# Four chained graph networks on one core: the written order of steps, one merge for the first five passes, one for the middle, one for the last six

## What is computed

```python
x = _layernorm(x + _L0_gnn_ref(x, adj, ...))
x = _layernorm(x + _L1_gnn_ref(x, adj, ...))
x = _layernorm(x + _L2_gnn_ref(x, adj, ...))
x = _layernorm(x + _L3_gnn_ref(x, adj, nodemask, ...))
```

## Time and profile before

| | |
|---|---|
| median of 3 runs | 1689.47 us (1687.17 to 1689.93) |
| span of the profiled execution, first to last instruction | 1687.2 us |
| TensorE, share of busy time | 96% |
| VectorE | 83% |
| ScalarE | 78% |
| GpSimd | 47% |
| mean granted TensorE clock | 0.995 of full speed |

### The profile page before, as it was taken

The page is one execution under the profiler, slowest core; times in us unless marked ns, Lnnn a source line. Parts: engine busy times, 40 slices in busy tenths (PEclk is TensorE's granted clock), DMA queues, the critical chain, the costliest instruction groups (busy, mean ns, idle before and its releaser), DMA issues.

```text
span 1687.2 us, 34433 instructions
## 1 busy us (share of the span) xinstructions
PE 1619.3 (96%) x12294; PEld 1343.7 (80%) x12294; DVE 1400.9 (83%) x3563; ACT 1314.6 (78%) x3147; POOL 790.3 (47%) x842
## 2 busy tenths in 40 slices
PE   8789999999999999999999999999999999999997
PEld 7568787887878788787887878888787888877776
DVE  5687888979789897989879798897978889797766
ACT  2568878887878888878887887878787888878766
POOL 3143544536454463544546354453645445354442
PEclk9899999999999999999999999999999999999999
DMA  3010100001010100101001010000101001000000
GB/s 95 20 42 1 30 26 17 27 14 42 14 30 14 28 28 14 30 26 30 14 20 36 14 31 26 18 26 14 43 13 30 25 17 27 14 26 14 13 1 20
DMA packets 84803, 40.97 MB, mean 24 GB/s; under 512 B 10629, under 2 KB 84634, under 8 KB 84634
## 3 DMA queue, kind: packets, MB, share of 16 engines
q1 hardware_dynamic: 84058, 38.62, 8.4%
q10 hardware_dynamic: 576, 0.15, 0.0%
HBM read 30.36 MB, written 8.39 MB: 23 GB/s over the span
## 4 chain that ended last, share of the span: by engine, by line
PE 82%; DVE 8%; ACT 7%; issue 1%; POOL 1%; SPq 0%; DMA 0%; POOLq 0%; DVEq 0%; ACTq 0%
PE RA L996 18%; PE RB L996 17%; PE Q L958 8%; PE RT L1193 8%; PE RT L958 4%; PE Q L1107 4%; PE Q L1124 3%; PE M L958 3%; PE Q L1140 2%; ACT x L553 2%; PE Q L1094 2%; PE Q L1090 2%; PE M L1157 2%; PE M L1152 2%; PE Q L1091 2%; PE M L1035 1%
## 5 line engine op out<-in xcount | busy, mean ns | idle before, releaser
L535 POOL TENSOR_TENSOR h_lo<-hT,h_hi 128x512 fp32r<-128x512 f32 (+1 forms) x163 | 205.9, 1264 | 561.0 <-ACT h_hi L636 488.3
L610 ACT ACTIVATE e_s<-Q,s_ng 128x128 f32<-128x128 f32 x1024 | 292.2, 398 | 42.2 <-DVE s_ng L803 42.1
L539 POOL TENSOR_TENSOR hd<-hT,nn 128x512 f32<-128x512 f32 x156 | 201.0, 1288 | 38.7 <-ACT nn L654 38.7
L811 DVE TENSOR_TENSOR p_s<-Q,adjTe 128x512 f32<-128x512 f32 x256 | 171.2, 684 | 15.5 <-PE Q L958 14.3
L803 DVE TENSOR_REDUCE s_ng<-Q 128x4 f32<-128x512 f32 x256 | 169.1, 682 | 14.0 <-PE Q L1107 12.3
L646 ACT ACTIVATE tr<-RA,b_rz 128x512 f32<-128x512 f32 (+1 forms) x160 | 113.7, 710 | 83.6 <-PE RA L996 83.6
L861 DVE SCALAR_TENSOR_TENSOR un<-tr,un 128x512 f32<-128x512 f32 (+1 forms) x164 | 115.1, 704 | 72.2 <-ACT un L650 71.7
L958 PE MATMUL Q<-ident,e_s 128*128 128x128 f32 x1024 | 154.0, 275 | 10.9 <-ACT e_s L610 10.8
L654 ACT ACTIVATE nn<-tr,wT 128x512 f32<-128x512 f32 (+1 forms) x164 | 118.0, 722 | 57.6 <-DVE tr L866 57.5
L958 PEld LDWEIGHTS Q<-ident,e_s 128*128 128x128 f32 x1024 | 122.3, 141 | 33.1 <-ACT e_s L610 16.6
L488 POOL TENSOR_TENSOR rs<-ve,half_neg 128x4 f32<-128x4 f32 x128 | 140.3, 1096 | 10.7
(11 more groups left out here) (237 smaller groups left out, 4429.2 us busy)
## 6 DMA issues: line engine op xcount, KB each, us to landing
...
adjc<-in_adj_dram SPq DMA_DIRECT2D x124, 4.0 KB, 2.1
xs<-in_x_dram SPq DMA_DIRECT2D x120, 16.0 KB, 1.8
...
```

Source lines behind the costliest of these rows:

```text
L535: pool.tensor_tensor(h_lo[g][:, c], hT[g][:, c], h_hi[g][:, c], ALU.subtract).then_inc(SG["h_lo"][g], 1)
L539: pool.tensor_tensor(hd[g][:, c], hT[g][:, c], nn[g][:, c], ALU.subtract).then_inc(SG["hd"][g], 1)
L610: ins = act.activation(e_s[:, j, c, :], Q[j][:, c * P:(c + 1) * P], ACT.Exp, bias=s_ng[:, j, c:c + 1])
L811: dve.tensor_tensor(p_s[:, j, :, :].rearrange("p (b h) q -> p b h q", b=2), Q[j][:, :].rearrange("p (b h q) -> p b h q", b=2, h=2), adjTe[ ...
```

## The change

No step, instruction, wait or transfer is added or removed. What changes is the written order of steps on TensorE, VectorE, ScalarE and GpSimd; SyncE's queue stays as it is. The old table had two strings for each engine, used in all 19 passes. The new one has three for each engine: one merges the steps of passes 0 to 4 together, so that a step of one pass may stand ahead of a step of the pass before; one is used for each of the passes 5 to 12; one merges passes 13 to 18. The three threads are divided into finer lanes, differently on each engine (`lane`): on TensorE the gated thread becomes R, I, Z and T; on the others the two sets of the gated thread become R and S, and maxima, products and parts of thread B get lanes of their own. Only steps that do something on an engine are in its lanes (`KINDS`). The steps that were put off near the end stay put off (`held_back`).

```diff
--- before.py
+++ after.py
@@ -48,15 +48,49 @@
 )
 LAG = 3
 
+HEAD, TAIL = 5, 13
+
 MERGE = dict(
-    tensor=("RRABBARARRBRARABRRRRAABAAARRARRRRAABRARARRRBRBBRBABBRARRRRARARRBBRRRRRRAAAARARABAARRRRBRRRRAAARRRRABBARAAARBBARRARRR",
...
+    tensor=(("BBBBBBBBABABAABBBABAAAAAABAAABAABABAABABABBAABAABABABAABABABAAAATAATARRRBABIZZAABABTABTARRRIAZZABATBTAARBRATRA"
...
 )
 
 
@@ -109,21 +143,84 @@
     return out
 
 
-def body_steps(merge):
-
-    out = []
-    for half in range(NG):
-        threads = dict(A=iter(attention_steps(half)), B=iter(first_third_steps(half)), R=iter(gated_steps(half)))
-        out += [(thread, *next(threads[thread])) for thread in merge[half]]
+THREADS = dict(A=[step for half in range(NG) for step in attention_steps(half)],
+               B=[step for half in range(NG) for step in first_third_steps(half)],
+               R=[step for half in range(NG) for step in gated_steps(half)])
+
+
+KINDS = dict(
...
+)
+
+
+def lane(engine, thread, g, kind):
+
+    if thread == "R" and engine == "tensor":
+        return {"r": "R", "r2": "R", "hn": "R", "in": "I", "z": "Z", "z2": "Z"}.get(kind, "T")
+    if thread == "R":
+        return "RS"[g]
+    if engine == "tensor":
+        return thread
+    if thread == "B":
+        if kind in ("x2", "x2_t", "l2_t", "l2_agg"):
+            return "C"
+        return "B" if kind not in ("adj_t", "l0_add", "x1") else "C" if engine == "vector" else "D"
+    return {"max": "M", "p": "P"}.get(kind, "A")
...
+def near_last(iters):
+    return [(iters - 2, NG - 1), (iters - 1, NG - 2)]
+
+
+def held_back(iters):
+
+    last, (third, second) = (iters - 1, NG - 1), near_last(iters)
...
+def sequence(engine, iters):
+
+    held = held_back(iters).get(engine, {})
+
+    head, body, tail = MERGE[engine]
+    blocks = [(range(HEAD), head)] + [(range(n, n + 1), body) for n in range(HEAD, TAIL)] + [(range(TAIL, iters + LAG), tail)]
+    for passes, merge in blocks:
+        threads = {name: iter([(n, (n - lag, g, kind, k)) for n in passes for lag, g, kind, k in steps if 0 <= n - lag < iters and (n - lag, g, kind, k) not in held])
+                   for name, steps in LANES[engine].items()}
+        for name in merge:
+            yield next(threads[name])
         assert all(next(left, None) is None for left in threads.values())
-    return out
...
@@ -165,20 +262,15 @@
 
         def program(eng, engine, steps, begun=(), first=None):
 
-            for kind in begun:
-                assert (0, kind) in [(lag, kind) for _, lag, g, kind, k in BODY[engine]]
-            held = {}
-            for it in range(ITERS + LAG):
-                for thread, lag, g, kind, k in BODY[engine]:
...
+            after = {}
+            for late, step in held_back(ITERS).get(engine, {}).items():
+                after.setdefault(step, []).append(late)
+            for n, step in sequence(engine, ITERS):
+                if (n == 0 and step[2] in begun) or step == first:
+                    continue
+                steps(*step)
+                for late in after.get(step, ()):
+                    steps(*late)
```

More of the change, by code:

```diff
@@ L118, in body_steps @@
         assert all(next(left, None) is None for left in threads.values())
[L119 to L124 removed]
+SLOTS = [(g, k) for lag, g, kind, k in THREADS["R"] if kind == "agg"]
 BEFORE = {slot: SLOTS[n - 1] for n, slot in enumerate(SLOTS)}
[L126 removed]
+LAG_OF = {(g, k): lag for lag, g, kind, k in THREADS["R"] if kind == "agg"}
@@ L307, in gnn_stack_kernel @@
         LAST = (ITERS - 1, NG - 1)
[L309 to L318 removed]
+        NEAR_LAST = near_last(ITERS)
         def parts(it, g, k):
```

92 lines of the change are left out of this document (63 added, 29 removed).

## The result

| | before | after |
|---|---|---|
| median of 4 runs, us | 1688.32 (1686.72 to 1689.93) | 1705.16 (1702.89 to 1706.32) |
| span of the profiled execution, us | 1687.2 | 1701.0 |
| TensorE busy, us | 1619.3 | 1622.7 |

The change makes the kernel slower: the ratio is 1.0099, 95% interval 1.0085 to 1.0114, that is 16.8 us. The forecast was 8 us shorter. The profiled execution of after is the shortest of its four, so its span shows 13.8 of the 16.8 us.

What follows compares the result with a forecast made beforehand. TensorE was taken as nearly full in the steady part, waiting on chains at both ends. Terms -5.6 + 2.4 + 1.4 - 5.0 - 1.4 = -8.2 us gave a span of 1679.0, with 2.3 added 1681.3, said as 1681; range 1671 to 1692.

Steps and rivals of the forecast that it cites:

- The sum is therefore over places where a wait goes or comes: Whole kernel: all steps, DMAs and waits stay, so only waits that go or come were summed.
- pass 0: Head: three moves shorten the chain of the first attention, -5.6 us; bounds -4 and -8.6.
- pass 2: Head: a_bin of the second four graphs, moved earlier, waits for its adjr load; +2.4 us, range 1.9 to 2.7.
- junctions 12 and 13: Two of ten body-like junctions: projections ahead of the first gated product hide the wait for h_lo, -0.1 us each.
- the 3 us: Slow-clock stretch from 78 to 85 us: up to 3 us more could go; left out of the sum.
- Body-like junctions: Ten junctions, x3 of graphs 4 to 13: o_ts wait replaced by hidden-state wait; +0.2 us in eight, +1.4 in all.
- Junctions of head and tail: Junctions 1, 2, 3, 14, 15: x3 starts at least 0.7 us sooner; -1.0 us each, -5.0 in all.
- Tail: Last x3: y4 goes ahead of un and tr, so it begins sooner; -1.4 us, bounds 0 and -1.4.
- R3: Mid pass: ScalarE's L0 block and normalisation ahead of agg_hi delay a product 1.5 us in ten passes; 1696 us, chance 0.12.

Runs made afterwards that it cites:

- head_first2: The kernel before with the new order in passes 0 and 1 alone; ratio 0.9973 to before, 4.6 us shorter.
- tail_only: The kernel before with the new order in passes 13 to 18 alone; ratio 1.0057 to before, 9.6 us longer.
- tail_pow: tail_only with GpSimd's adjTe, x1b and t_d replaced by powers of few columns lasting about as long; 1695.61 us, ratio 1.0035 to before.
- ends16: head_first2 with the new order also in passes 16 to 18; 1679.20 us, ratio 0.9945 to before.

## Why the prediction was wrong

The step that failed is the one that stands ahead of all terms: "The sum is therefore over places where a wait goes or comes". Terms were booked for pass 0, for pass 2 and for the junctions alone. What lies between the junctions was put at nothing, as if every step lasted as long in its new place as in its old one and TensorE came to every other product as before. Term by term (junction k, the x3 of pass k of the data, lies at the end of pass k+1 of the program):

| part | forecast, us | measured, us |
|---|---|---|
| pass 0 | -5.6 | -3.7 to -4.6 |
| pass 2 | +2.4 | +2.2 |
| from the first hT to that at 427, junctions 1 to 3 | -3.0 | +4.0 |
| passes 5 to 12, eight junctions | +1.6 | +5.2 |
| passes 13 to 15 to hT at 1486, junctions 12 and 13 | -0.2 | +14.1 |
| from there to the end, junctions 14 and 15, last x3 | -3.4 | -5.8 |

**Pass 0, -5.6.** Right in the mechanism and at the low end of its bounds. The product of the values moved from 94.78 to 88.94, but some 1.4 us of that are the clock's; at like clock the order wins 3.7 to 4.4, and head_first2 kept 4.6 by its ratio. The granted clock from 50 to 100 us is 0.93 instead of 0.88, with a new slow stretch (0.63 from 92 to 96). Since kernels of one order differ as much (0.94 and 0.97 up to 115 us in before and tail_only), leaving the 3 us out of the sum was right; here the trace agrees with what the prediction cites.

**Pass 2, +2.4.** Right. a_bin waited 2.77 us for adjr, whose issue moved from 104.59 only to 99.13 while agg_lo moved from 104.84 to 98.52. The load was there 2.86 us after its issue: between the prediction's estimate of 2.6 us, whose section in the Trainium skill is on transfers that GpSimd issues, while SyncE issues this one, and the 3.0 to 3.8 of the earlier trace rows. At either clock the kernels with the new pass 2 stand 2.2 us behind those without it at the first hT (-3.6 against -5.8, -1.5 against -3.7).

**Body-like junctions, +0.14 each.** The junction itself was read rightly: o_ts 1.05 out, hT 0.71 in, and 0.43 of small ones, +0.1 in all. VectorE's sum from hT to nm is the same (4.69 us, before 4.72), and from hT to x3 it takes 5.1 us instead of 4.9, the 0.2 of the forecast. What failed is that nothing was booked for the rest of the pass. There dinv0m, held by t_d, makes the wait of 0.49 for hT; the pass costs 0.6, the body 5.2. With the three GpSimd steps replaced the loss is gone.

**Junctions of head and tail, -1.0 each.** Here too x3 comes sooner behind hT, by 0.3, 0.4 and 0.4 us at junctions 1 to 3 and by 0.7 and 0.4 at 14 and 15 (4.58, 4.53, 4.24, 4.23 and 4.24 us, before 4.91, 4.92, 4.65, 4.92 and 4.65); at four of the five less than the 0.7 forecast. The loss lies between the junctions, where nothing was booked. From the first hT to 427 the head lost 4 us instead of winning 3. With the three steps cut the loss between the same marks is 1.6, so a good half of it is holds. The rest is not settled. Passes 13 to 15 lose 14.1 us. The prediction did not look at them apart from the junctions at all; their merge was new too, and I took them for copies of the steady pass. TensorE's waits there are, besides the 2.42 at 1304.45:

```profile
1435.60 0.70 PE L1097 MATMUL M<-nat,sel 128*128 128x112 f32 x4 [1.11 <-DVE nat L838]
...
1444.51 0.47 PE L1079 MATMUL RA<-agg_hi,comp_hi 128*128 128x512 f32 x1 [1.70 <-DVE agg_lo L939]
...
1480.37 0.47 PE L1079 MATMUL RA<-agg_hi,comp_hi 128*128 128x512 f32 x1 [1.75 <-DVE agg_lo L939]
```

(tail_only.) Each stands behind a VectorE step that is drawn out while GpSimd steps run: a_c 2.43 us instead of 0.60 (beside hd and x1b), x from xin 3.08 instead of 1.11 (beside h_lo and hd), x from y 2.91 instead of 1.11 (beside x1b and hd). The four waits are 7 of the 14.1 us. In tail_pow they are 1.03, gone, 1.67 and 0.91, in the same order. The one that stays whole stands behind the x beside h_lo and hd, the two steps that no kernel here replaced (tail_only, then tail_pow: VectorE, GpSimd, and TensorE's wait in tail_pow):

```profile
1439.49 3.08 DVE L797 TENSOR_SCALAR x<-xin,mv,rs 128x128 f32<-128x128 f32 x4
...
1439.47 1.27 POOL L618 TENSOR_TENSOR h_lo<-hT,h_hi 128x512 fp32r<-128x512 f32 x1 [5.39 <-ACT h_hi L719]
1440.70 1.27 POOL L622 TENSOR_TENSOR hd<-hT,nn 128x512 f32<-128x512 f32 x1
...
1438.67 3.08 DVE L799 TENSOR_SCALAR x<-xin,mv,rs 128x128 f32<-128x128 f32 x4
...
1443.70 0.47 PE L1081 MATMUL RA<-agg_hi,comp_hi 128*128 128x512 f32 x1 [1.67 <-DVE agg_lo L941]
```

So holds by h_lo and hd can make part of the 7.4 us that stay in passes 13 to 15, but this is read from rows and not shown by a run; how much is the order itself stays open.

**Tail, -1.4.** Right in mechanism and size. From the hT ahead of it to the last x3 before needs 4.31 us, after 2.85:

```profile
1621.97 0.69 DVE L879 SCALAR_TENSOR_TENSOR hT<-hd,nn 128x512 f32<-128x512 f32 x1
...
1637.27 0.69 DVE L962 SCALAR_TENSOR_TENSOR hT<-hd,nn 128x512 f32<-128x512 f32 x1
...
1640.12 1.65 ACT L636 ACTIVATE x<-y,nm,rs 128x128 f32<-128x128 f32 x4 [0.97 <-DVE y L969]
```

(The first row is of before, to be read with the earlier trace rows.) Passes 16 to 18 win more than the 2.4 booked for junction 15 and this x3: 4.7 us by the ratios (ends16 against head_first2, 0.9945 and 0.9973), 4.6 in the trace of ends16. Where the rest comes from was not looked into. The last x3 of after is at 1640.12, 13.8 us later than in the earlier trace rows, and from there to the end both kernels need 60.9 us.

**Rivals.** The time fell past R3, 1696, but its mechanism is not there: in the steady pass of after TensorE has no wait between 613.70 and 688.93, so ScalarE's L0 block ahead of agg_hi costs nothing. What was missing is a rival in which durations change. The trace of before had it. In this timeline (VectorE, GpSimd) nm, 4 columns wide, lasts 1.22 us beside hd, where the nm of the earlier trace rows takes 0.15:

```profile
592.79 1.22 DVE L710 SCALAR_TENSOR_TENSOR nm<-mv,rs 128x4 f32<-128x4 f32 x1
...
592.72 1.27 POOL L539 TENSOR_TENSOR hd<-hT,nn 128x512 f32<-128x512 f32 x1
```

This happens 29 times in before. In the pass shown TensorE does not wait behind it: its one wait up to 690.31 is the 0.39 for on_ts, which ScalarE makes. So the old order has its collisions on steps that TensorE does not wait for, as far as the waits show. The new order has them on dinv0m, x, a_c and hT, and TensorE waits behind these.
